# The order of 1,439 steps of a two-layer kernel, rewritten from its head to its end

## The reference

```
x = x + softmax(mask(layernorm(x) @ ctx.T / 16)) @ ctx            # layer 0, attention
x = x + sum over the 2 best of 8 experts: w * (silu(h@Wg)*(h@Wu))@Wd,  h = layernorm(x)
x = x + (top-54 softmax of (coef * (h @ Wq.T) @ ctx.T)) @ ctx @ Wo.T   # layer 1, attention
x = x + bitlinear(gelu(bitlinear(layernorm(x), w1)), w2)          # 8-bit activations, ternary weights
```

## Time and profile before

| | us |
|---|---|
| median of 3 runs (lowest, highest) | 411.09 (410.61, 411.27) |
| the profiled execution | 412.79 |
| its span | 410.7 |
| PE busy | 356.3 (87%) |
| DVE busy | 291.6 (71%) |
| ACT busy | 189.4 (46%) |
| POOL busy | 59.2 (14%) |

### The profile page before, as it was taken

One profiled execution on the slowest core, in us unless ns is written; L12 is line 12 of the kernel. 1 busy time (PEld: TensorE's weight loads), 2 busy tenths in 40 slices (PEclk: granted clock), 3 DMA queues, 4 the chain that ended last, 5 costly groups with the idle time before them and its releaser, 6 DMA issues. The chain is left out here.

```text
span 410.7 us, 6718 instructions
## 1 busy us (share of the span) xinstructions
PE 356.3 (87%) x2108; PEld 284.7 (69%) x2114; DVE 291.6 (71%) x713; ACT 189.4 (46%) x344; POOL 59.2 (14%) x136
## 2 busy tenths in 40 slices
...
GB/s 231 380 286 43 248 375 140 288 183 205 287 301 296 272 273 95 77 141 269 266 315 299 260 308 263 214 102 81 285 60 109 13 95 28 1 161 71 53 14 53
DMA packets 70811, 76.41 MB, mean 186 GB/s; under 512 B 5356, under 2 KB 69496, under 8 KB 70776
## 3 DMA queue, kind: packets, MB, share of 16 engines
...
...
## 5 line engine op out<-in xcount | busy, mean ns | idle before, releaser
L995 PE MATMUL GU<-xgT,wg_ring 128*128 128x128 f32 x480 | 58.8, 277 | 4.4 <-issue 4.0
L995 PEld LDWEIGHTS GU<-xgT,wg_ring 128*128 128x128 f32 x480 | 56.4, 192 | 8.4 <-issue 6.4
L677 ACT ACTIVATE pT<-T 128x512 f32<-128x512 f32 (+1 forms) x64 | 31.8, 511 | 50.8 <-PE T L931 46.9
L948 PE MATMUL A<-pT,v_sb 128*128 128x128 f32 (+1 forms) x416 | 54.9, 290 | 0.0
L948 PEld LDWEIGHTS A<-pT,v_sb 128*128 128x128 f32 (+1 forms) x416 | 53.7, 207 | 1.4 <-issue 0.3
L1278 DVE MAX8 cand_h<-fold 128x8 f32<-128x801 f32 x56 | 54.4, 981 | 0.0
L917 PE MATMUL S<-k_sb,xT 128*128 128x400 f32 (+2 forms) x128 | 50.9, 538 | 1.4 <-ACT xT L662 0.8
L917 PE MATMUL S<-k_sb,qT 128*128 128x400 f32 (+2 forms) x128 | 48.3, 513 | 2.8 <-ACT qT L735 1.6
L944 PE MATMUL A<-v_sb,pT 128*128 128x256 f32 (+1 forms) x208 | 48.9, 380 | 0.0
L931 PE MATMUL T<-ident,row 128*128 128x128 f32 (+1 forms) x208 | 34.8, 298 | 14.8 <-DVE row L1314 8.3
L1290 DVE MATCH_REPLACE8 fold<-cand_h,fold 128x801 f32<-128x801 f32 x48 | 46.8, 976 | 0.0
...
## 6 DMA issues: line engine op xcount, KB each, us to landing
...
k_sb<-ctxT SPq DMA_DIRECT2D x16, 400.0 KB, 4.9
...
```

The costliest lines, as they stand in the source:

```text
L677: act.activation(pT[0:r, i % NPT, :, :].rearrange("p a s -> p (a s)")[:, 0:w], t_bank("pT", *key)[0:r, 0:w], ACT.Copy).then_inc(pTe_done, 1)
L948: mm = pe.matmul(A_bank[:, o * P:(o + 1) * P], v[0:r, a, o * P:(o + 1) * P], pT[0:r, j, a, :], start=m == 0 and o == 0, stop=m == NMC - 1 ...
L995: mm = pe.matmul(gu_bank(*key)[:, a * F + f * P:a * F + (f + 1) * P], wg_ring[:, w % NWG, a, k, f * P:(f + 1) * P], cols[:, k, :], start=k ...
```

## The change

Only the text ORDER is changed. It holds the same 1,439 steps, each once, and no function is touched, so every engine executes the same operations on the same data in another sequence. The first 177 steps are those of another order of this kernel; the rest is new as well. The table of steps says little to a reader, so two of its lines stand for it:

```diff
-ldx.0 stats.1.0 ldx.2 ldx.3 ldk.1.0.1 ldx.1 ldk.1.0.2 ldk.1.0.0 ldk.1.0.3 aggr.1.0 var.1.0 rstd.1.0 stats.1.2 wload.1
+ldx.0 stats.1.0 aggr.1.0 var.1.0 rstd.1.0 norm.1.0 xT.1.0 xTe.1.0 ldx.2 ldk.1.0.3 ldk.1.0.1 s1.0.1 ldk.1.0.2 s1.0.2
...
```

More of the change, by code:

```diff
@@ L77 @@
[L77 to L101, removed]
```

178 lines of the change are left out of this document (102 added, 76 removed).

## The result

The changed kernel is slower: 415.38 us median of 6 runs (413.93 to 416.45) where the kernel before has 411.18 (410.25 to 414.1) beside it; ratio 1.0085, 95% interval 1.0044 to 1.0126. By the ratio that is +3.5 us, the two medians lie 4.2 apart. I had forecast -1.9. The profiled execution took 416.45 us for a span of 413.8.

A forecast was written before the change was run, and what follows sets the result against it. Full engines change by stage: TensorE from 20 to 178 us, VectorE from 178 to 384. Terms -2.2 - 0.7 - 0.2 + 0.8 + 0.2 + 0 + 0.2 = -1.9 gave a 409.2 us median, range 406.0 to 413.5.

The forecast's parts named there:

- The start: First four score chunks: later w1 load removes a key wait and raises the clock sooner, -2.2 us.
- my lower bound of 0.6: Smallest gain allowed at the kernel's start, 0.6 us, if the clock rises no sooner than before.
- my terms up to there: Start -2.2, first expert group and numbering -0.7, way to first search -0.2, VectorE in second expert group +0.8 us.
- VectorE in group 1: Second group of experts, 178 to 255 us: waits for `silu` grow from 3.0 to 3.8 us, +0.8.
- Gathers: After group 1's last product: first update wants the second gather, fewer loads beside them; +0.2 us, bounds -1.4 and +1.7.
- The rest of the search: Search from 255 to 384 us, waits other than for gathers: no change, 0, bounds -1.2 and +2.
- The tail: Kernel's end: `h4T.4` and `fin.5` cost, earlier `dn.6` helps; together +0.2 us, bounds -0.3 and +0.9.
- The rivals: Whole kernel: all kept 406.5 (0.17), group 1 swallows it 411.1 (0.09), clock no sooner 410.8 (0.10), slower 413.9 (0.24).
- Slower: VectorE reaches gated steps of group 1 before their data, lost leads become waits: +2.8 us, 413.9; chance 0.24.
- its lost leads of group 1: Second expert group on VectorE: 1.1 us at `mul.1.1`, 1.8 at `mul.1.2`, 1.9 at `mul.1.12`, turned into waits.
- its own mark: The slower case decides once VectorE's waits for `silu` and gathers exceed 7.5 us.

The follow-up runs named there:

- e13: The kernel before, unchanged, run once more for a second profile; no ratio given, the fourth score chunk ends at 17.25 us.
- e2: Order of before up to the last product of group 1 (`mul.1.14`), then the changed order; ratio to the kernel before 1.0080.
- e8: Only the first 177 steps of the changed order (w1 and w2 loaded later), then the order of before; ratio to the kernel before 1.0147.
- e11: The changed kernel plus idle TensorE transposes ahead of `wo.6` and `pT.3.7.0` in the tail; ratio to the kernel before 1.0049.
- e1: Changed order up to the last product of group 1 (`mul.1.14`), then the order of before; ratio to the kernel before 0.9928.
- e15: The kernel before, with loads from `ldk.3.2.2` on waiting until group 1's fourth gather has landed; ratio to the kernel before 1.0029.
- e3: The changed kernel plus idle TensorE transposes ahead of `xT.3.4`, `wo.6` and `pT.3.7.0`; ratio to the kernel before 0.9995.
- e9: The changed kernel, with `ldv.3.3.0` and all SyncE loads behind it waiting until the fourth gather has landed; ratio to the kernel before 0.9918.
- e10: The changed kernel plus 32 idle TensorE transposes ahead of `xT.3.4` alone; ratio to the kernel before 1.0013.
- e12: The changed kernel measured once more, nothing altered; ratio to the kernel before 1.0080.

## Why the prediction was wrong, step by step

**The start, forecast -2.2.** In the first pair of traces it came as forecast or better (-3.3 at `s1.0.3`; TensorE's first chunks in one row without a wait, beside the earlier trace rows):

```profile
9.09 11.43 PE L918 MATMUL S<-k_sb,xT 128*128 128x400 f32 x28 [0.78 <-ACT xT L663]
```

Yet it was mostly chance: in the four other profiles of the old start it ends at 17.25 to 17.5, so the order is worth 0.4 us there, below my lower bound of 0.6 (0.8 us if the first trace is counted with them). The trace I predicted from had a late clock and a late key load, and it was itself an execution of 412.79 where the median is 411.09. The Trainium skill (TensorE: Matmul & The Clock Gate, Part 1) says that the number of slow first matmuls varies from run to run. The traces agree: `s1.0.3` ends at 17.25 in e13 and at 17.38 in e2, where the first trace of the same start has 19.80. I had taken this variation as a bound of the gain, when it spoke against the base I measured the gain from.

**The head as a whole** still wins. `mul.1.14` ends at 254.6, 255.0, 252.7, 254.6 and 257.6 in the five profiles with the old head (mean 254.9) and at 250.4 to 255.0 in ten with the new head (mean 252.5; all of the table but e8 and e11), a gain of about 2.4 us where my terms up to there add up to -2.3 (-2.2 - 0.7 - 0.2 + 0.8), and e1 confirms it in time (-0.72 per cent, 3 us). The sum is right by luck, for it does not lie at the start: 0.4 us are there, and 2.0 by the end of `pairH.0` (means of the same profiles). In e13 TensorE pauses 2.43 us at 163 and the clock is at 0.52 until 166.5; e15 has a pause of 3.42 at the same place; the first trace of before has none, yet its head ends at 254.6 like that of e13. So this pause alone does not explain it, and what the new head wins by stays open.

**VectorE in group 1, +0.8.** I forecast 3.8 us of waits with one of 1.2 to 1.8 ahead of the second `mul`; measured were 2.7, in two pieces of 1.46 and 1.28. The second piece stands ahead of the second `mul`, as forecast (1.28 again in e1, e3, e9, e10 and e12). The first stands ahead of the first `mul`, which waited 0.36 before and which I had not named, and the two waits of about a microsecond that I kept, at `mul.1.5` and `mul.1.14`, are gone. So the wait that I had named came, the others did not, and the sum was 1.1 too high. `pairH.0` began at 175.00, as written.

**Gathers, +0.2 (bounds -1.4 and +1.7): the step that failed.** I wrote that before three loads of 0.4 to 0.5 MB were issued beside the gathers and "after only one is, so they may land sooner". The first half holds; these are SyncE's loads in the kernel before:

```profile
258.16 0.38 SPq L508 DMA_DIRECT2D v_sb<-ctx  x1
258.59 0.51 SPq L490 DMA_DIRECT2D k_sb<-ctxT  x1
259.14 0.47 SPq L508 DMA_DIRECT2D v_sb<-ctx  x1
```

They are issued just ahead of the first gather (259.27), and by their semaphores the first four gathers landed 5.8, 6.5, 5.6 and 3.4 us after their issue. The second half is wrong. In the kernel after only one such load is issued beside the first two gathers (256.51), but SyncE issues two value loads and a key load between 258.30 and 259.77, just ahead of the fourth at 260.45: the gathers landed in 3.9, 3.8, 7.4 and 6.2 us, where the fourth needed 2.7 at most with those loads held back (e9). So the loads did not go, they moved from the first of these gathers to the last two. Place in ORDER does not show this: `ldv.3.3.0` stands behind `upd.4.1` there, but SyncE waits ahead of it only for the products that free its buffer, and issued it 8.4 us before `upd.4.1` began. And I priced the first update's wait and not the third's, which needs the fourth gather. The term was +2.3 instead of +0.2 (3.7 us of waits for 1.4), outside its bounds. The Trainium skill (DMA: Bandwidth & Descriptors, SWDGE vs HWDGE vs iDMA) says that GpSimd's transfers and SyncE's feed different queues in each DMA engine, and that the engine takes them in turn. e9 agrees in so far as the gather lands sooner when SyncE's loads are held back; no run shows the turns.

**The rest of the search, 0 (bounds -1.2 and +2).** The leads of `x3`, `gabs` and `fin` were counted, that of `pairL.4` was not; the chain fourth gather, `norm.3.4`, `xT.3.4`, `qT.4`, scores of tile 4 had its slack eaten by the gather and then by the clock. It measured +2.5: 2.8 us for tile 4 and 0.8 for `fin`, against 1.1 of other waits before. The clock is what made the 2.8: e3 and e10 take it away without bringing `xT.3.4` sooner, with the gathers as late as ever. Here too a step failed, a term put at nothing: TensorE's pause and the clock behind it were not in the sum. This term and the one for gathers make 4.8 us, and the rest is longer by some 4.6 (4.0 in e12), against 3.7 at my outermost bounds.

**The tail, +0.2 (bounds -0.3 and +0.9).** It measured +1.7, and +0.6 to +1.7 over all traces with the new tail. I weighed `h4T.4` and `dn.6` and passed over `exp3.7`, which moved ahead of `aTe.6` on ScalarE; its price is again the clock (24.3 us when filled, below the old order's 24.9).

**The rivals.** "Slower" had the sign, and with 413.9 nearly the size, but its mechanism was not the one: its lost leads of group 1 cost nothing, and only its last part, 0.9 us at the first update, lay near the place where the loss arose. Nor was its own mark reached: VectorE's waits for `silu` and gathers came to 6.4 us, not over 7.5. Neither my forecast nor any rival let the clock fall in the middle of the kernel, though the trace of before had it at 0.88 in the mean of 255:384. I had read that number as harmless everywhere, because it was so in that order.
